# The experts' short down products, taken once for two pairs of tiles

## The reference

```
h = layernorm(x) * (1 + cb) + sb
router = h @ gate_w.T                     # 8 experts, the best two of each token are kept
hid_e = silu(h @ fc1_e.T) * (h @ fc2_e.T) # 176 hidden columns for each expert e
y     = sum over the token's two experts of weight_e * (hid_e @ proj_e.T)
shared = silu(h @ s1.T) * (h @ s2.T) @ sproj.T   # 704 hidden columns
out   = x + gb * (y + sigmoid(h @ sgate) * shared)
```

## Time and profile before

| | |
|---|---|
| Median of three runs | 398.69 us (393.92 to 399.45) |
| Profiled execution: span from first to last instruction | 394.7 us |
| Time of the profiled execution around its span | none is recorded; the span is 0.2% above the fastest run |
| TensorE matmul busy | 368.1 us, 93% |
| VectorE / ScalarE / GpSimd busy | 241.7 / 144.6 / 146.4 us |
| Granted TensorE clock, mean | 0.996 of full speed |
| Expert stage, 250 to 370 us: TensorE / VectorE / GpSimd busy | 120.0 / 64.3 / 71.7 us of 120 |
| First and last indirect store of the experts' results | start at 279.62 and 369.52 us |

### The profile page before, as it was taken

The page is one execution under the profiler, slowest core; times in us unless marked ns, Lnnn a source line. Parts: engine busy times, 40 slices in busy tenths (PEclk is TensorE's granted clock), DMA queues, the critical chain, the costliest instruction groups (busy, mean ns, idle before and its releaser), DMA issues.

```text
span 394.7 us, 9939 instructions
## 1 busy us (share of the span) xinstructions
PE 368.1 (93%) x3837; PEld 230.1 (58%) x3838; DVE 241.7 (61%) x578; ACT 144.6 (37%) x303; POOL 146.4 (37%) x252
## 2 busy tenths in 40 slices
PE   1989789999989989899999999999999999999996
PEld 1445365648454846565674484485666666665465
DVE  3068675689668956975549186207555555555377
ACT  3296514754474452226204331103333333332110
POOL 8503200620061006201727016731467777766200
PEclk9999899999999999999999999999999999999999
DMA  7960300000000000007972007241233333311297
GB/s 243 290 207 2 110 3 4 2 2 3 4 0 3 3 3 2 4 2 250 269 247 96 15 1 219 85 135 55 84 106 102 114 100 96 108 43 44 64 354 240
DMA packets 29901, 36.66 MB, mean 93 GB/s; under 512 B 4567, under 2 KB 26530, under 8 KB 29860
## 3 DMA queue, kind: packets, MB, share of 16 engines
q1 hardware_dynamic: 26452, 27.58, 23.7%
q0 software_dynamic: 3408, 8.51, 6.3%
HBM read 23.31 MB, written 13.68 MB: 94 GB/s over the span
## 4 chain that ended last, share of the span: by engine, by line
PE 80%; DVE 6%; ACT 5%; issue 3%; DMA 3%; POOL 0%; SPq 0%; DVEq 0%; POOLq 0%; ACTq 0%
PE at_ps L1820 13%; PE work L1446 9%; PE work L1495 6%; PE at_ps L1461 5%; PE at_ps L1446 5%; PE at_ps L1531 4%; PE work L1843 4%; PE work L1845 3%; PE work L1633 3%; PE work L1683 2%; PE at_ps L1495 2%; PE work L1461 2%; PE at_ps L1804 2%; PE o_even L1586 2%; DMA hs<-in_wmod 2%
## 5 line engine op out<-in xcount | busy, mean ns | idle before, releaser
L1820 PE MATMUL at_ps<-arena 128*128 x156 | 54.5, 472 | 0.0
L657 POOL DMA_INDIRECT ys_tokens<-er_pos,goal_u x39 | 41.7, 1070 | 33.7 <-DVE er_pos L1369 23.9
L586 POOL TENSOR_TENSOR sq<-sq,sg 128x512 f32<-128x512 f32 x8 | 10.0, 1276 | 101.0 <-issue 101.0
L628 POOL DMA_INDIRECT xs_sorted<-h2tok,pos_u x32 | 31.6, 989 | 37.0 <-DVE pos_u L993 18.8
L1820 PEld LDWEIGHTS at_ps<-arena 128*128 128x128 f32 x156 | 26.6, 190 | 14.9 <-issue 6.6
L899 ACT ACTIVATE arena<-at_ps 128x176 f32<-128x176 f32 x39 | 12.4, 318 | 58.8 <-PE at_ps L1820 56.5
L1369 DVE SCALAR_TENSOR_TENSOR er_pos<-work,goal,sq 128x256 f32<-128x256 f32 x39 | 17.2, 480 | 22.0 <-PE work L1850 21.0
L1446 PE MATMUL work<-h2T,sup_sb 128*128 128x512 f32 x56 | 25.7, 598 | 0.0
L1196 DVE COPY_PREDICATED arena<-causal,at_ps 128x512 f32<-128x512 uint32 x32 | 20.6, 721 | 7.3 <-PE at_ps L1531 7.3
L1349 DVE TENSOR_TENSOR arena<-at_ps,arena 128x176 f32<-128x176 f32 x39 | 13.3, 342 | 18.4 <-ACT arena L899 15.9
L1461 PE MATMUL at_ps<-sdn_sb,hs 128*128 128x256 f32 x100 | 22.1, 380 | 0.0
(11 more groups left out here) (281 smaller groups left out, 818.6 us busy)
## 6 DMA issues: line engine op xcount, KB each, us to landing
h2tok<-xs_sorted SPq DMA_DIRECT2D x40, 131.5 KB
arena<-ys_tokens SPq DMA_DIRECT2D x8, 512.0 KB, 7.7
arena<-in_e_up SPq DMA_DIRECT2D x8, 352.0 KB
x_sb<-in_x SPq DMA_DIRECT2D x4, 512.0 KB, 7.5
out_rows<-x_sb SPq DMA_DIRECT2D x16, 128.0 KB, 4.0
sup_sb<-in_s_up SPq DMA_DIRECT2D x2, 640.0 KB, 4.7
xs_sorted<-state SPq DMA_DIRECT2D x2, 526.0 KB
xs_sorted<-state SPq DMA_DIRECT2D x8, 131.5 KB
```

The costliest lines, as they stand in the source:

```text
L628: g.indirect_dma_start(out=xs_dram, out_offset=bass.IndirectOffsetOnAxis(ap=pos_u[:, k, t:t + 1], axis=0), in_=h2tok[:, t, :], in_offset=N ...
L657: g.indirect_dma_start(out=ys_dram, out_offset=bass.IndirectOffsetOnAxis(ap=goal_u[:, i:i + 1], axis=0), in_=yout[:, q % 2, u, :], in_offs ...
L1820: ins = t_.matmul(at_ps[2 + u % 2][:, 0:2 * FE], xT[:, u % 2, k * P:(k + 1) * P], eup[:, bass.ds(e, 1), k, :].rearrange("p a n -> p (a n)" ...
```

## The change

The full down products stay one pair at a time. Those of the second pair of each two go to columns 256 to 511 of the same two banks, without the start flag. The short products move to a new function `down_short`, which runs behind the second pair's full products and does all four tiles: row half 0, row half 1 of the first pair, then of the second. Only then is `down_full` raised, once for two pairs. So VectorE's gains and evacuations come in fours (`out_rows`: four `row_gains` instructions, then four `evac_y`), in every second pair's place. The gains get four slots (in `xn`), the odd tiles' copied weights four (all of `xn2`), and TensorE keeps four expert registers of the last group. `down` waits for `y_out` only at the first pair of two. `yout` keeps four slots; GpSimd's and SP's lists are not edited. The last run of short products has three tiles.

```
-        tail_odd = xn2[:, 0:2, :]
+        tail_odd = xn2[:, :, :]
...
-        row_step, row_gain = sq[:, 0, 0:HID], sq[:, 1, :].rearrange("p (a n) -> p a n", a=2)
+        row_step, row_gain = sq[:, 0, 0:HID], xn
...
-            def odd_rows(q, w, e):
-
-                act.wait_ge(down_full, q - 1)
+            def odd_rows(d, w, e):
+
+                act.wait_ge(down_full, d)
...
-                        if first and u < 4:
+                        if first:
                             copy_odd_rows(u // 2, e[u])
                         else:
-                            odd_rows(q0 + u // 2, u // 2, e[u])
+                            odd_rows(d0 + u // 4 - 1, u // 2, e[u])
...
-                if not isinstance(i, int) or i:
+                if u % 4 == 0 and (not isinstance(i, int) or i):
                     dve.wait_ge(y_out, i)
                 dve.wait_ge(goal_ready, i + 2)
                 for t in range(2):
-                    v.scalar_tensor_tensor(out=row_gain[:, t, :], in0=row_step, scalar=goal[:, (u // 2) % XPAIRS, t, 2:3],
+                    v.scalar_tensor_tensor(out=row_gain[:, u % 4 + t, :], in0=row_step, scalar=goal[:, (u // 2) % XPAIRS, t, 2:3],
                                            in1=rows[:, 0, GB, :], op0=ALU.mult, op1=ALU.add).then_inc(gain_ready, 1)
-            def evac_y(i0, q0, u):
-
-                dve.wait_ge(down_full, q0 + u // 2 + 1)
+            def evac_y(i0, d0, u):
+
+                dve.wait_ge(down_full, d0 + u // 4 + 1)
                 dve.wait_ge(gain_ready, i0 + u + 2 - u % 2)
-                v.scalar_tensor_tensor(out=yout[:, (u // 2) % 2, u % 2, :], in0=work[u % 2][:, 0:HID],
-                                       scalar=goal[:, (u // 2) % XPAIRS, u % 2, 1:2], in1=row_gain[:, u % 2, :],
+                c = slice((u // 2) % 2 * HID, (u // 2) % 2 * HID + HID)
+                v.scalar_tensor_tensor(out=yout[:, (u // 2) % 2, u % 2, :], in0=work[u % 2][:, c],
+                                       scalar=goal[:, (u // 2) % XPAIRS, u % 2, 1:2], in1=row_gain[:, u % 4, :],
                                        op0=ALU.mult, op1=ALU.mult).then_inc(y_out, 1)
             def y_slot_free(i0, u):
@@ -1376,34 +1377,36 @@
                 if not isinstance(i0, int) or i0 or n:
                     dve.wait_ge(ys_stored[u % 4], i0 * 4 + n)
-            def group(i0, q0, tiles=EGRP, first=False):
+            def out_rows(i0, d0, u, tiles=4):
+
+                for n in range(u, u + tiles, 2):
+                    row_gains(i0 + n, n)
+                for n in range(u, u + tiles):
+                    y_slot_free(i0, n)
+                    evac_y(i0, d0, n)
+
+            def group(i0, q0, d0, tiles=EGRP, first=False):
                 for u in range(0, tiles, 2):
                     expert_h(i0 + u, u)
                     if u or not first:
                         evac_hT(q0 + u // 2 - 1, (u // 2 - 1) % XPAIRS)
-                        row_gains(i0 + u - 2 if u else i0 - 2, (u - 2) % EGRP)
                     if u + 1 < tiles:
                         expert_h(i0 + u + 1, u + 1)
-                    for t in range(2):
-                        if u:
-                            y_slot_free(i0, u - 2 + t)
-                            evac_y(i0, q0, u - 2 + t)
-                        elif not first:
-                            y_slot_free(i0 - EGRP, EGRP - 2 + t)
-                            evac_y(i0 - EGRP, q0 - XPAIRS, EGRP - 2 + t)
+                    if u == 4:
+                        out_rows(i0, d0, 0)
+                    elif u == 0 and not first:
+                        out_rows(i0 - EGRP, d0 - XPAIRS // 2, 4)
             dve.wait_ge(y_ready, 2 * NBLK)
             steps.did(v.tensor_tensor(row_step, rows[:, 1, GB, :], rows[:, 0, GB, :], ALU.subtract))
             steps.sync()
-            group(0, 0, first=True)
+            group(0, 0, 0, first=True)
             with dve.Fori(1, ESLOTS // EGRP - 1) as grp:
-                group(grp * EGRP, grp * XPAIRS)
-            group(ESLOTS - EGRP, ESLOTS // 2 - XPAIRS, tiles=ETILES - ESLOTS + EGRP)
+                group(grp * EGRP, grp * XPAIRS, grp * (XPAIRS // 2))
...
-            row_gains(ETILES - 1, EGRP - 2)
-            y_slot_free(ESLOTS - EGRP, EGRP - 2)
-            evac_y(ESLOTS - EGRP, ESLOTS // 2 - XPAIRS, EGRP - 2)
+            out_rows(ESLOTS - EGRP, (ESLOTS // 2 - XPAIRS) // 2, 4, tiles=3)
...
-                at_least(pe, y_out, i, 0)
+                if w % 2 == 0:
+                    at_least(pe, y_out, i, 0)
+                c = slice(w % 2 * HID, w % 2 * HID + HID)
                 for t in range(tiles):
                     main = edn_odd if t else edn[:, 0, :, :]
-                    t_.matmul(work[t][:, 0:HID], hTe[:, w % 2, t * P:(t + 1) * P],
-                              main[:, bass.ds(e[t], 1), :].rearrange("p a n -> p (a n)"), start=True, stop=False)
-                ins = t_.matmul(work[0][:, 0:HID], hTe[0:FE1, w % 2, 2 * P:3 * P],
-                                edn[0:FE1, 1, bass.ds(e[0], 1), :].rearrange("p a n -> p (a n)"), start=False, stop=True)
-                if tiles == 2:
+                    t_.matmul(work[t][:, c], hTe[:, w % 2, t * P:(t + 1) * P],
+                              main[:, bass.ds(e[t], 1), :].rearrange("p a n -> p (a n)"),
+                              start=(w % 2 == 0), stop=False, skip_group_check=True)
+
+            def down_short(q, w, e, tiles=4):
+
+                if tiles == 4:
                     pe.wait_ge(odd_ready, q + 1)
-                    r = slice(CHUNK, CHUNK + FE1)
-                    ins = t_.matmul(work[1][:, 0:HID], hTe[r, w % 2, 2 * P:3 * P], tail_odd[r, w % 2, :],
-                                    start=False, stop=True)
+                else:
+                    pe.wait_ge(odd_ready, q)
+                r = slice(CHUNK, CHUNK + FE1)
+                for a in range(2):
+                    c = slice(a * HID, a * HID + HID)
+                    ins = t_.matmul(work[0][:, c], hTe[0:FE1, a, 2 * P:3 * P],
+                                    edn[0:FE1, 1, bass.ds(e[2 * a], 1), :].rearrange("p a n -> p (a n)"),
+                                    start=False, stop=True, skip_group_check=True)
+                    if 2 * a + 1 < tiles:
+                        ins = t_.matmul(work[1][:, c], hTe[r, a, 2 * P:3 * P], tail_odd[r, (w - 1 + a) % XPAIRS, :],
+                                        start=False, stop=True, skip_group_check=True)
                 ins.then_inc(down_full, 1)
...
+                def short_behind(u):
+                    if u == 4:
+                        down_short(q0 + 1, 1, e[0:4])
+                    elif u == 0 and before is not None:
+                        down_short(q0 - 1, XPAIRS - 1, before)
...
                     pair_behind(down, u)
+                    short_behind(u)
...
-            down(ETILES - 1, EPAIRS - 1, XPAIRS - 1, previous()[0:1], tiles=1)
+            down(ETILES - 1, EPAIRS - 1, XPAIRS - 1, previous()[2:3], tiles=1)
+            down_short(EPAIRS - 1, XPAIRS - 1, previous(), tiles=3)
```

More of the change, by code:

```diff
@@ L906, in _, with group @@
             ereg = [act.alloc_register(f"odd_expert{u}") for u in range(EGRP)]
-            def odd_rows(q, w, e):
-                act.wait_ge(down_full, q - 1)
+            def odd_rows(d, w, e):
+                act.wait_ge(down_full, d)
                 copy_odd_rows(w, e)
             def copy_odd_rows(w, e):
-                a.activation(tail_odd[CHUNK:CHUNK + FE1, w % 2, :], edn[0:FE1, 0, bass.ds(e, 1), :].rearrange("p a n -> p (a n)"),
+                a.activation(tail_odd[CHUNK:CHUNK + FE1, w, :], edn[0:FE1, 0, bass.ds(e, 1), :].rearrange("p a n -> p (a n)"),
                              ACT.Copy).then_inc(odd_ready, 1)
-            def group(i0, q0, tiles=EGRP, first=False, last=False):
+            def group(i0, d0, tiles=EGRP, first=False, last=False):
                 act.load(ereg, texp_u[0:1, bass.ds(i0, EGRP)])
@@ L931, in _ @@
             with act.Fori(1, ESLOTS // EGRP - 1) as grp:
-                group(grp * EGRP, grp * XPAIRS)
-            group(ESLOTS - EGRP, ESLOTS // 2 - XPAIRS, tiles=ETILES - ESLOTS + EGRP, last=True)
+                group(grp * EGRP, grp * (XPAIRS // 2))
+            group(ESLOTS - EGRP, (ESLOTS // 2 - XPAIRS) // 2, tiles=ETILES - ESLOTS + EGRP, last=True)
             for f in range(EARLY_UP, FTS):
@@ L1398, in _ @@
             steps.sync()
-            group(0, 0, first=True)
+            group(0, 0, 0, first=True)
             with dve.Fori(1, ESLOTS // EGRP - 1) as grp:
-                group(grp * EGRP, grp * XPAIRS)
-            group(ESLOTS - EGRP, ESLOTS // 2 - XPAIRS, tiles=ETILES - ESLOTS + EGRP)
+                group(grp * EGRP, grp * XPAIRS, grp * (XPAIRS // 2))
+            group(ESLOTS - EGRP, ESLOTS // 2 - XPAIRS, (ESLOTS // 2 - XPAIRS) // 2, tiles=ETILES - ESLOTS + EGRP)
             evac_hT(EPAIRS - 1, XPAIRS - 1)
-            row_gains(ETILES - 1, EGRP - 2)
```

(12 more changed lines are left out.)

## The result

The changed kernel takes 399.03 us in the median of 22 runs (395.38 to 403.82), the kernel before 395.73 us in 22 runs beside them (393.04 to 399.45). The ratio is 1.0066, 95% interval 1.0036 to 1.0097: slower by 2.6 us (1.4 to 3.8). The interval excludes 1, and the loss is well under the 2% that the prediction took as what a measurement can tell. The ratio is made from undisturbed runs alone, so it isn't the quotient of the medians. The forecast time, 400.0, is 1.0 off. But the forecast difference was +1.3, and the median of three runs on which it stood, 398.69, was itself 3 us above the 395.73 of the 22. Two errors in opposite directions make the time look better than the working was.

The account below looks back on a forecast made before the run. GpSimd and TensorE stand at the same 4.83 us pace; the change speeds up only TensorE, so GpSimd bounds. A later start, 17 pitches and four stores put the last store +1.3 us; 398.69 + 1.3 = 400.0 us, range 394 to 403.

Parts of the forecast that it names:

- the 2% that the prediction took as what a measurement can tell: Whole kernel: about 2%, 8 us, is what a measurement tells from no change.
- the median of three runs: Kernel before: 398.69 us, to which the forecast difference of 1.3 was added.
- TensorE's part: Short products: 1.25 us for two pairs against 1.62, 0.37 saved; ten runs give 3.7 us.
- The late start: GpSimd's first result store: at 284.28, 4.7 us later than before, as pair 0's results wait for pair 1's short products.
- 0.2 late: VectorE: four gains end at 298.29, so the first evacuation starts 0.2 us behind the 298.09 it could have.
- I take the middle, 4.78, and keep both: GpSimd's pitch a pair, between 4.73 and 4.83: 17 pitches of 4.78 take 81.3 us to pair 17's first store.
- own work: GpSimd before the change: its 4.83 us pitch, dispatch gaps included, is its own and equals TensorE's.
- never free: GpSimd before the change: its 0.78 us gap is dispatch and not waiting, so it has no room.
- one gain of 0.44 in some six runs, +2.6: GpSimd's targets beside VectorE's gains: expected overlap, giving 402.6 us, inside the range.
- the rival in which the gains lock GpSimd out: Targets beside gains: the full 1.74 us in each of eight runs gives 413.9 us, slower; chance 10%.
- The held VectorE: At `y_slot_free`: GpSimd's run falls 0.27 us behind TensorE's each time, holding VectorE; most of TensorE's 3.7 is given back.
- TensorE, if early, waits in front of the shared down product. The shift passes through in full.: Tail after the last store: steps follow one another as before, so the last store's 1.3 us delay reaches the end.

Follow-up runs that it names:

- a_g2: The changed kernel with GpSimd's target arithmetic done once for two pairs (seven instructions in place of ten): 398.63 us, ratio 1.0064.
- a_y8: The changed kernel with eight result slots in SBUF in place of four: 399.3 us, ratio 1.0082.
- a_nogain: The changed kernel without the rows of gains from the fifth tile on: 397.28 us, ratio 1.0012.
- a_warm: The changed kernel with four unused products of 512 columns in front of the shared down product: 399.09 us, ratio 1.0061.
- a_early: The changed kernel with only the first run undone, pairs 0 and 1 each on their own: 401.27 us, ratio 1.0105.
- a_best: The changed kernel with target arithmetic merged for two pairs, and pairs 16 to 18 and tile 38 each on their own: 394.2 us, ratio 0.9970.
- the repeat: The changed kernel once more, unedited: 399.54 us, ratio 1.0081.
- a_split0: The changed kernel with only the last run undone, pair 18 and tile 38 each on their own, targets not merged: 398.56 us, ratio 1.0038.
- a_each: The changed kernel with short products back behind each pair's own full products, results still gathered in fours: 401.14 us, ratio 1.0108.

## Why the forecast was right, and where its working was not

**TensorE's part was right.** The four tiles' short products run from 325.37 to 326.43, 1.06 us, and the period in a_g2 is 9.26. Against 2 x 4.83 that is 0.40 less, where 0.37 was forecast. The rule of the Trainium skill, "TensorEngine Tiling (Array Packing)", Tiling Modes, Key Properties, that changing the tiling mode drains the array, agrees with this: one change less for two pairs. For the kernel's time it told nothing: the saving is there, and the change is slower.

**The late start was right.** Forecast 13.85 from first up product to first store, measured 13.64. Four gains took 1.66 for 1.74, and the evacuation wasn't 0.2 late: at the run shown it starts at 326.58, 0.15 behind the short products.

**The pitch was mis-sized, at the step "I take the middle, 4.78, and keep both".** GpSimd's own pitch is 4.71, just under the low bound of 4.73. The prediction called the 4.83 of the earlier trace rows GpSimd's "own work" and GpSimd "never free"; that reading was wrong. The 4.83 was TensorE's, and GpSimd had room, some of it at the end. Alone that would have given 17 x 4.71 = 80.1, 1.2 less than forecast, and no loss at all. But what the forecast left to its range, "one gain of 0.44 in some six runs, +2.6", came true: 17 pitches took 83.7. Of the 3.6 above GpSimd's own, 2.1 are stretched targets (0.48 at 286.70 and at 316.49, 0.67 in the pair at 360.32, the rest at 306.36 and 326.39), 0.6 stretched stores (0.25 at 344.43, 0.22 at 353.00, less at 295.90 and 334.93), 0.4 the wait before 309.38, and 0.3 each two gaps without a cause in the profile, before 294.51 and before 346.99. All that is stretched has gains beside it, 2.7 in all. So the rival in which the gains lock GpSimd out was the better account of the pitch, at its small price and not its large one. Stage: -0.2 for the start, +2.4 for the pitches, against +1.3 forecast, is +3.5.

The Trainium skill, "SBUF — State Buffer", Who interferes with whom, says that a VectorE instruction with two SBUF inputs contends with a GpSimd instruction that reads SBUF. The trace agrees, 0.58 to 1.06, and so do the gains taken away. The indirect stores are held as well, if less: in a_y8 second stores of 0.98 take 1.24 in some pairs, and in a_nogain no store behind the first is longer than 1.09.

**The held VectorE was right as a wait and wrong as a cost.** It is held 6 times for 5.9 us, and takes 1.94 at once where a landing took 4.2 for 2.5; eight slots take all of that away and give back less than 0.8. It isn't always free: the one late landing of a_nogain cost 0.84.

**The tail was wrong, at the step "TensorE, if early, waits in front of the shared down product. The shift passes through in full."** I saw the wait, 3.3 us, and costed it at nothing. What it costs is the clock behind it: the 20 products take 7.45 for 4.58, on the path that sets the end, and the tail is 2.2 longer. a_warm, which does nothing but fill that idle time, takes it away.

**The sum.** +3.5 and +2.2 are 5.7 in one execution, 2.7 and 2.3 in the other; the timed runs give +2.6 (1.4 to 3.8), and +2.4 at equal clock by the estimate. Single runs point to the reason: with a mean granted clock of 1.0, which a fallen tail doesn't leave, the change still took 395.4 to 397.6 (four runs) and the kernel before 392.7 to 394.5 (18 runs of three comparisons). So the stage's loss is there without the tail's, and the tail's is not in every run; in how many it is isn't shown. The forecast of +1.3 was half of what came, and 400.0 was near through the high median below it. Part of that is luck: with its own pitch corrected to 4.71 the working gives +0.1, and the rest came from the gains and the tail, which it had put in the range and at nothing.

## What to carry to other kernels

Before an engine is sped up, build the pitch of each engine downstream of it, dispatch gaps counted as work: an engine at 37% busy over the span, 71% in its own stage, was within 0.12 us a pair of being the bound, and it turned a saving of 3.7 us into a loss. Gathering results into larger runs costs a longer start and a later end, so keep the last group small (an early first group alone gained nothing here, in a_early), and lighten the consumer first (a_best does both). An engine that waits before the last stretch isn't free where its clock can fall: price the work that follows it at both levels.

## What the runs showed of the hardware that I had not expected

- An idle TensorE of 3.3 us (3.5 in the repeat) was followed by 20 products of 7.4 us for 4.6, an idle of 1.4 to 2.7 in a_g2, a_split0 and a_nogain was not, and one of 2.3 in a_each was (6.3 us for the 20), like those of 3.5 in a_early (6.3) and 5.9 in a_y8 (6.9). Idle length alone doesn't tell.
- The spread between runs of one kernel goes with the mean granted clock: over 34 runs of the kernel before in one comparison, 392.7 to 393.7 us at 1.0, 395.4 to 397.5 at 0.990, 399.8 to 400.6 at 0.981, about 0.3 us for each 0.001. A difference of 2 us between two medians can be that.
- GpSimd's indirect stores are held by the gains as well, if little: 0.98 becomes 1.10 in the kernel before and 1.24 in a_y8; first stores of 1.09 become 1.31 in the change. The landing of one goes from 2.1 to 4.2 us within one execution.
- VectorE started twice in a_g2 more than 1 us after what it waited for had ended (310.19 above), idle for 0.81 and 1.15 of it, with no cause in the profile.
- The short products of the two row halves run side by side: that of the odd tile starts 0.01 us behind that of the even tile (325.37 and 325.38).
